# Keys projected by kv head, and the twelve NF4 chunks placed 1-8-3 instead of 2-8-2 around the heads

## The reference

```
q = rope(layernorm(x) @ Wq)      32 query heads of 128
k = rope(ctx @ Wk), v = ctx @ Wv  8 kv heads of 128, 4 query heads share one
w = softmax(where(mask, 30*tanh(q.k*MULT/30), -1e30))
x = x + (w @ v) @ Wo
g = layernorm(x)
x = x + (silu(g @ dq(w1).T) * (g @ dq(w2).T)) @ dq(w3).T      hidden size 1376
```

## Time and profile before

| what | us |
|---|---|
| median of 3 runs (lowest, highest) | 897.48 (897.24, 898.55) |
| the profiled execution, its own time | 897.72 |
| its span, first to last instruction | 895.9 |
| TensorE busy | 814.8 (91%) |
| VectorE busy | 738.5 (82%) |
| ScalarE busy | 436.6 (49%) |
| GpSimd busy | 368.9 (41%) |
| mean granted TensorE clock | 0.975 of full |

### The profile page before, as it was taken

The page is one execution under the profiler, slowest core; times in us unless marked ns, Lnnn a source line. Parts: engine busy times, 40 slices in busy tenths (PEclk is TensorE's granted clock), DMA queues, the critical chain, the costliest instruction groups (busy, mean ns, idle before and its releaser), DMA issues.

```text
span 895.9 us, 10645 instructions
## 1 busy us (share of the span) xinstructions
PE 814.8 (91%) x3806; PEld 645.6 (72%) x3806; DVE 738.5 (82%) x857; ACT 436.6 (49%) x521; POOL 368.9 (41%) x208
## 2 busy tenths in 40 slices
PE   3588798799899999999999999999768999998998
PEld 2466586677677787677777777777546788887886
DVE  8799978599899989999999998898787799895120
ACT  0044466465565565665665566555642365462100
POOL 3445428534634735645536527435001335444000
PEclk9999899899999999999999999999888999999999
DMA  8455564632333432432523433322101311303210
GB/s 323 135 155 145 167 201 106 183 107 80 112 106 83 140 100 72 147 83 71 167 71 87 146 92 97 113 70 80 59 1 33 103 48 54 106 1 104 56 59 36
DMA packets 61940, 91.82 MB, mean 102 GB/s; under 512 B 6720, under 2 KB 28352, under 8 KB 61888
## 3 DMA queue, kind: packets, MB, share of 16 engines
q1 hardware_dynamic: 61888, 91.14, 34.5%
HBM read 51.00 MB, written 19.14 MB: 78 GB/s over the span
## 4 chain that ended last, share of the span: by engine, by line
PE 51%; DVE 25%; issue 9%; DMA 5%; ACT 5%; POOL 3%; SPq 1%; POOLq 0%; DVEq 0%; ACTq 0%
PE bank L454 5%; PE bank L456 5%; PE bank L455 5%; PE bank L545 3%; PE bank L490 3%; PE bank L491 3%; PE bank L474 3%; PE bank L492 3%; PE bank L472 3%; PE bank L473 3%; ACT nfp L690 3%; DVE nfa L856 3%; PE trp L461 3%; PE avp L556 2%; DVE nfx L856 2%
## 5 line engine op out<-in xcount | busy, mean ns | idle before, releaser
L1141 POOL TENSOR_TENSOR qT<-cs_loop,sw 128x512 f32<-128x512 f32 x58 | 82.0, 1414 | 234.2 <-DMA sw<-cs_loop 234.2
L856 DVE SCALAR_TENSOR_TENSOR nfv<-nfp,nfv 128x1408 f32<-128x1408 uint8 x70 | 134.4, 1920 | 18.8 <-ACT nfp L690 16.8
L738 ACT ACTIVATE bank<-bank 128x512 f32<-128x512 f32 x64 | 37.2, 582 | 176.7 <-PE bank L545 176.7
L690 ACT ACTIVATE nfp<-nfv,bnd 128x1408 uint8<-128x1408 f32 x75 | 107.2, 1465 | 23.0 <-POOL nfv L1157 11.4
L856 DVE SCALAR_TENSOR_TENSOR nfa<-nfp,nfa 128x1408 f32<-128x1408 uint8 x56 | 100.3, 1790 | 14.3 <-ACT nfp L690 13.7
L490 PE MATMUL bank<-woh,ath 128*128 128x512 f32 x256 | 109.8, 429 | 0.0
L690 ACT ACTIVATE nfp<-nfa,bnd 128x1408 uint8<-128x1408 f32 x75 | 106.7, 1464 | 5.9 <-POOL nfa L1157 3.6
L472 PE MATMUL bank<-xh,wqh 128*128 128x512 f32 x256 | 106.0, 414 | 0.0
L491 PE MATMUL bank<-wol,ath 128*128 128x512 f32 x256 | 103.6, 405 | 0.0
L492 PE MATMUL bank<-woh,atl 128*128 128x512 f32 x256 | 103.6, 405 | 0.0
L474 PE MATMUL bank<-xh,wql 128*128 128x512 f32 x256 | 101.3, 396 | 0.0
(11 more groups left out here) (130 smaller groups left out, 1775.4 us busy)
## 6 DMA issues: line engine op xcount, KB each, us to landing
sw<-cs_loop SPq DMA_DIRECT2D x116, 128.0 KB, 2.3
stage<-wq_pieces SPq DMA_DIRECT2D x32, 256.0 KB, 2.9
stage<-wo_pieces SPq DMA_DIRECT2D x32, 256.0 KB, 3.0
stage<-dq_scratch SPq DMA_DIRECT2D x32, 256.0 KB, 3.1
sw<-cs_start SPq DMA_DIRECT2D x44, 128.0 KB, 2.3
ks_scratch<-qT SPq DMA_DIRECT2D x16, 256.0 KB, 2.5
vs_scratch<-vst SPq DMA_DIRECT2D x16, 256.0 KB, 4.1
kcur<-ks_scratch SPq DMA_DIRECT2D x16, 256.0 KB, 3.7
```

Source lines behind the costliest of these rows:

```text
L690: nc.scalar.activation(nfp[:, n % 2, :], nf_bufs(c)[0][:, :], ACT.Sign, bias=bnd[:, i:i + 1])\
L856: op = nc.vector.scalar_tensor_tensor(acc[:, :], nfp[:, n % 2, :], STEPS[i], acc[:, :], ALU.mult, ALU.add)
```

## The change

It is one change with these parts:

1. **Keys by kv head.** Wk is laid out by kv head; a piece holds one head. Units run over all eight heads with tokens 0 to 511, then over all eight with tokens 512 to 1023. The first unit needs five pieces and takes them one at a time; unit u < 8 then waits for one more piece each.
2. **Splits of the first 28 pieces.** hi is made by ScalarE (`first_hi`), lo by GpSimd for thirteen pieces (`FIRST_POOL`) and by VectorE for fifteen (`first_low`). Most lo of Wk and ctx's second half stand behind a `rope_parts` or a `rope` in the engines' programs.
3. **Order around the keys.** The eight transposes move to u = 10 to 15 and v = 0, 1; mask tables to u = 8; layer norm to u = 5 to 7.
4. **NF4 placement.** No chunk in the keys. Chunk 0 (now a quarter of w3) at v = 0 to 12; chunks 1 to 8 (w1, w2) in heads 0 to 7; chunks 9, 10, 11 (w3) in the FFN at n = 2 to 22 with one more buffer `nfy`. w3's chunks are cut by blocks of columns (`W3_RUNS`), and stored in two DMAs each. SP stores chunk 0 at v = 14 (ahead of `query_swap(4)`), chunk 9 ahead of `weights_in(15)`.
5. **Hidden's hi on ScalarE**, one unit late (`hidden_hi(n - 1)` behind `silu(n)`), instead of on VectorE.
6. **Down** waits for `h_lo` tile by tile.

```diff
+W3_RUNS = [[(0, 5), (21, 27)], [(5, 11), (27, 32)], [(11, 16), (32, 38)], [(16, 21), (38, 43)]]
...
+            nfy = sb("nfy", [128, CH], f32, ffn)
...
+        FIRST_POOL = (0, 3, 6, 8, 10, 12, 14, 16, 18, 20, 22, 24, 26)
...
         def nf_values(v):
-            if v < 4:
-                return 0, range(9 + 6 * v // 4, 9 + 6 * (v + 1) // 4)
-            return 1, range(15 * (v - 7) // 9, 15 * (v - 6) // 9) if v >= 7 else range(0)
+            return range(15 * v // 13, 15 * (v + 1) // 13) if v < 13 else range(0)
...
         def nf_ffn(n):
-            chunk, m = (10, n - 2) if n < 10 else (11, n - 11)
-            return chunk, range(15 * m // 8, 15 * (m + 1) // 8) if 0 <= m < 8 else []
+            return [divmod(k, 15) for k in range(45 * (n - 2) // 21, 45 * (n - 1) // 21)] if n >= 2 else []
...
(SP)
-            for n in range(12):
+            for n in range(5):
                 first_piece(n)
+            sp.dma_start(tab[:, :, :], table_d).then_inc(tab_in, 16)
             sp.dma_start(mt8[:, :], mask_t).then_inc(mask_in, 16)
-            sp.dma_start(tab[:, :, :], table_d).then_inc(tab_in, 16)
-            for n in range(12, 16):
+            for n in range(5, 16):
                 first_piece(n)
...
             for v in range(16):
-                if v == 4:
-                    nf_load(nf_first[:, CH:2 * CH], 1)
+                if v == 13:
+                    nf_load(1)
+                if v == 14:
+                    nf_store(0)
...
+            sp.wait_ge(nf_out, nf_stored(NKV))
+            nf_load(NKV + 2)
             for n in range(4, 2 * HT):
-                if n == 14:
-                    nf_load(nf_first[:, 4 * CH:5 * CH], 11)
-                if n == 16:
-                    nf_store(dq3[:, 2 * CH:3 * CH], 10)
+                if n == 15:
+                    nf_store(NKV + 1)
+                if n == 17:
+                    nf_load(NKV + 3)
                 weights_in(n)
...
(TensorE)
             for u in range(NK):
-                c, half, kvl = u // 8, u % 8 // 4, u % 4
+                half, kv = u // 8, u % 8
+                if u > 0:
+                    split(pe, 5 + u if half == 0 else 16)
                 wait(pe, cs_done, u - 1)
...
+                for k in range(KT):
+                    if u == 0:
+                        split(pe, k + 2)
...
-                if n == 0:
-                    pe.wait_ge(h_lo, 2 * HT)
+                pe.wait_ge(h_lo, units_of(n))
...
(ScalarE)
+            for n in range(16):
+                first_hi(n)
+            for u in range(10, NK):
+                first_token_hi(u - 10)
+                if u >= 12:
+                    first_hi(u + 4)
...
                 silu(n)
-                chunk, bounds = nf_ffn(n)
-                for i in bounds:
-                    nf_above_bound(chunk, i)
+                if n > 0:
+                    hidden_hi(n - 1)
+                for c, i in nf_ffn(n):
+                    nf_above_bound(NKV + 1 + c, i)
+            hidden_hi(2 * HT - 1)
+            for c, i in nf_ffn(2 * HT):
+                nf_above_bound(NKV + 1 + c, i)
...
(VectorE)
+            for n in (1, 2, 4):
+                first_low(n)
...
             for u in range(NK):
                 rope_parts(u, u % 2, tab[:, 0:2, :])
+                if u < 6:
+                    first_low(5 + 2 * u)
+                if u == 5:
                     dve.wait_ge(x_in, 16)
                     for b in range(4):
                         nc.vector.bn_stats(stat[:, b, :], y[:, b, :])
+                if u == 6:
                     ln_moments(0, range(B), 4)
+                if u == 7:
                     ln_rstd(0, range(B))
                     normalise(0, nrm)
                     normalise(1, nrm)
+                if u == 8:
+                    mask_tables()
+                if u >= 10:
+                    token(u - 10)
+                if u in (13, 14):
+                    first_low(2 * u - 9)
+            nf_prepare(0)
...
             def hidden(n):
...
-                dve.wait_ge(h_done, n + 1)
-                nc.vector.tensor_copy(hh[:, t, half * 512:(half + 1) * 512], hf[:, n % 2, :]).then_inc(h_hi, 1)
...
-                if n in (1, 10):
-                    nf_prepare(10 + n // 10)
+                if n in (1, 7, 14):
+                    nf_prepare(NKV + 1 + n // 7)
...
(GpSimd)
-            for n in range(0, 12, 2):
+            for n in (0, 3, 6):
                 first_low(n)
...
+                for n in {0: (8,), 2: (10,), 3: (12,), 5: (14,), 12: (16,), 13: (18,)}.get(u, ()):
+                    first_low(n)
+                if u == 5:
                     power(0, range(B))
+            first_low(20)
+            nf_normalise(0)
+            for n in (22, 24, 26):
                 first_low(n)
...
             for u in range(AHEAD):
                 query_rope(u)
                 if u in (1, 3):
                     for n in (28 + u - 1, 29 + u - 1):
                         low(n % 4, woh0[:, n % 4, :], wol0[:, n % 4, :], n)
+                if u == 3:
+                    nf_rescale(0)
+            nf_normalise(1)
...
-                if n in (9, 18):
-                    nf_rescale(10 + n // 18)
+                if n in (9, 16):
+                    nf_rescale(NKV + 1 + n // 16)
+            nf_rescale(NKV + 3)
```

More of the change, by code:

```diff
@@ L199, in split @@
         def split(eng, n):
-            if isinstance(n, int) and n <= WO0:
-                wait(eng, piece_lo, (n + 1) // 2)
-                wait(eng, piece_lo_dve, n // 2)
+            if n <= WO0:
+                early_pool = len([m for m in range(n) if m in FIRST_POOL])
+                wait(eng, piece_lo, early_pool)
+                wait(eng, piece_lo_dve, n - early_pool)
             else:
-                eng.wait_ge(piece_lo, n - WO0 // 2)
+                eng.wait_ge(piece_lo, n - WO0 + len(FIRST_POOL))
         def source(n):
@@ L401, in head @@
                 if last:
-                    wait(sp, nf_out, 16 * 9)
+                    sp.wait_ge(nf_out, nf_stored(NKV - 1))
                     for n in range(4):
                         weights_in(n)
-                if last:
-                    nf_load(nf_first[:, 3 * CH:4 * CH], kv + 3)
+                    nf_load(NKV + 1)
             def weights_in(n):
@@ L726, in _ @@
                 nc.scalar.activation(vst[:, v % 4, :], prj2[v % 2][:, :], ACT.Copy).then_inc(v_copied, 1)
-                chunk, bounds = nf_values(v)
-                for i in bounds[0:1]:
-                    nf_above_bound(chunk, i)
-                for i in bounds[1:]:
-                    nf_above_bound(chunk, i)
+                if v < 2:
+                    first_token_hi(6 + v)
+                for n in range(20 + 2 * v, 22 + 2 * v) if v < 4 else ():
+                    first_hi(n)
+                for i in nf_values(v):
+                    nf_above_bound(0, i)
                 if 9 <= v < 13:
@@ L986, in _ @@
                     rope_parts(NK + u, u % 2, csq[:, :, :])
-                for i in bounds[1:]:
-                    nf_add(chunk, i)
+            nf_prepare(1)
             def mask(j):
@@ L1107, in _ @@
                 hidden(n)
-                if n in (1, 10):
-                    nf_prepare(10 + n // 10)
-                chunk, bounds = nf_ffn(n)
-                for i in bounds:
-                    nf_add(chunk, i)
+                if n in (1, 7, 14):
+                    nf_prepare(NKV + 1 + n // 7)
+                for c, i in nf_ffn(n):
+                    nf_add(NKV + 1 + c, i)
+            for c, i in nf_ffn(2 * HT):
+                nf_add(NKV + 1 + c, i)
             for n in range(HT):
@@ L1206, in head @@
                     if b == 7 and not last:
[L1207 to L1211 removed]
+                        nf_normalise(kv + 2)
+                    if b == 0 and kv > 0:
+                        nf_rescale(kv)
                     if not last and b < 4:
@@ L1256 @@
              for w in (w1, w2)]
-    parts.append(np.pad(w3.reshape(2, 128, 2 * HID).transpose(1, 0, 2).reshape(128, 4 * HID),
-                        ((0, 0), (0, NFW - 4 * HID))))
-    nf = np.split(np.concatenate(parts, axis=1), 12, axis=1)
-    nf_first, nf_rest = (np.concatenate([nf[c] for c in cs], axis=1) for cs in ([8, 9, 0, 10, 11], range(1, 8)))
+    by_row = np.pad(w3.reshape(2, 128, 43, BLK).transpose(1, 0, 2, 3), ((0, 0), (0, 0), (0, 1), (0, 0)))
+    cols = [[b for lo, hi in runs for b in range(lo, hi)] for runs in W3_RUNS]
+    third = [by_row[:, :, (c + [43])[:11]].reshape(128, CH) for c in cols]
+    nf = np.concatenate([third[0]] + parts + third[1:], axis=1)
     mask = f(np.asarray(mask_1x1xSxS2_bk0)[0, 0].T)
```

283 lines of the change are left out of this document (128 added, 155 removed).

## The result

The changed kernel takes 909.26 us (median of four runs, 907.06 to 911.54) against 897.36 (897.11 to 898.55) before: a ratio of 1.013, 95% interval 1.0098 to 1.0162. The forecast was 900.2, with a range of 889 to 909. The direction was right, the size was not, and the time lies just outside the range.

What follows compares the result with a forecast made beforehand. TensorE was busy 91% and VectorE 82%, so the question was where TensorE waits; in the FFN, VectorE. A gain of 12.8 by head 0 and a loss of 15.5 in the FFN gave +2.7: 900.2 us, range 889 to 909.

Steps and rivals of the forecast that it cites:

- The start: Keys, values and early queries: first matmul about 7.1, first value 71.1, last query ending 138.9, a gain of 14.6 us.
- The second transpose comes at +19.8: Head 0: that transpose comes 19.8 us after the last early query, before 18.1; 1.8 goes back, 12.8 stays gained.
- Heads: The heads themselves: costed at nothing, since the steps are the same and TensorE sets them.
- VectorE is the matter: FFN: VectorE's work from `hf(2)` sums to 122.8 us and sets the down stage's start, a loss of 15.5.
- upper bound of 22: FFN: the largest loss foreseen, 22 us, with slower additions and the full 6 us wait at chunk 9's store.
- Start-up of the first Signs adds 1.5: FFN's beginning: the first Signs' start-up adds 1.5 us to VectorE's sum of work.
- The store of chunk 9: FFN, SP ahead of `weights_in(15)`: TensorE stands 5 to 6 us, VectorE about 4; cost between 0 and 6.
- The tail: FFN's end: the last three bounds follow unit 21, ahead of w3's split; the down stage starts when VectorE is through, 842.4.
- some 12 us after TensorE's last gate product: Sign of being right: the down stage starts that long after the FFN's last gate product.
- VectorE idle in the FFN by over 10 us: Sign of being wrong: VectorE was forecast without idle from n = 6 on.
- The FFN absorbs the third chunk: Rival, VectorE at n = 2 to 22: FFN loss under 12.8, likely 6, kernel faster at 890.7 us; chance 0.28.
- The start gains little: Rival: lows behind ropes, SP's order and the table load leave a gain of 6, not 12.8: 907 us; chance 0.17.

Runs made afterwards that it cites:

- e7: Changed kernel with the load of x behind the swap of key unit 1 and chunk 0's load behind that of unit 5: 911.23 us.
- e6: Changed kernel with SP's store of chunk 0 behind the whole value loop instead of at v = 14: 904.63 us.
- e1: Changed kernel with GpSimd's normalise of chunk 9 ahead of the `hl` of unit 1 instead of behind it: 903.99 us.
- e5: Changed kernel with the reorderings of e1, e2 and e3 together: 891.41 us, ratio 0.9929 to the kernel before.
- e8: Changed kernel without the fifteen bounds of the last chunk, so a quarter of w3 isn't quantised: 899.78 us.
- e4: Changed kernel with the casts of `hidden` back on VectorE, directly behind `hf` (part 5 undone): 909.91 us.
- e2: Changed kernel with SP's store of chunk 9 behind the load of piece 16 instead of ahead of 15: 905.26 us.
- e3: Changed kernel with w3's first two splits ahead of the last three bounds, on ScalarE and VectorE: 905.67 us.
- e10: Changed kernel with the edits of e5 and e6, and the 45 bounds spread over n = 2 to 21 instead of 22: 889.98 us.

## Why the prediction was wrong, point by point

**The start: right.** First matmul, unit 4, first value and last early query were within 1.1 us of the working. The gain at the last early query was 12.7 and not the 14.6 forecast: 1.0 because it came later than said, the rest by the late reading of the time before. The swap behind `x` landed at 24.35, where 23.3 was said, and e7 shows the queueing.

**Head 0: mis-sized.** The step "The second transpose comes at +19.8" measured 23.5 (139.9 to 163.40). Before, it was 18.9 and not 18.1 (152.6 to 171.53), so 4.6 went back where 1.8 was counted. The chain was named, SP's block at v = 14 and a first Sign 10.7 after the last query. The Sign came 14.8 after it (154.73). What was priced too low is the late `swap(4)`: GpSimd's 5.86 wait stands ahead of the normalise. e6 removes it, and TensorE's wait falls from 9.24 to 1.84. The gain at that transpose was 8.1, not 12.8.

**Heads: costed at nothing, gave 4.2 back.** From that transpose to `hf(2)` it took 541.8 before and 537.6 after. That made the total at `hf(2)` 12.3, near the 12.8 forecast, by two errors that cancel: that agreement is luck. In e1 to e5 and e8, with the same code up to there, it took 536.0 to 538.1, so the 4.2 is more than their spread; of the kernel before there is one trace. That trace places most of it: the lead is 8.3 at the fifth transpose and 11.9 at the ninth (232.37 before, 220.44 after), and in between TensorE waited 1.12 and 2.85 for VectorE's `nrm` before (221.56, 232.37) and not at all for it after. Why VectorE was late there was not tried.

**FFN: the step that failed.** "VectorE is the matter", and the sum of 122.8 for its work with 1.5 for the start-up and 4 for n = 12, gave a loss of 15.5; it was 22.4, just past the upper bound of 22. (That bound was added up wrongly: 15.5, 6.8 for slower additions and 2 for the full 6 make 24.3, and the 22.4 lies inside that.) It was wrong on both sides, too much work and too little waiting:

- *VectorE's work* was 109.4 busy, not 122.8. The 42 additions in the stretch take 79.56, 1.89 each, against 58.34 / 28 = 2.08 before. Alone they would take 42 x 1.67 = 70.1, so contention is 9.4 there, not the 16 and 4 counted. The sum also had 45 at 1.63, but the first of each chunk is another operation, and the three took 3.2 together. The copies on ScalarE move `hl` by a unit, and many then meet no addition: with the copies back on VectorE (e4) the same 42 take 87.9, 2.09 each.
- *"Start-up of the first Signs adds 1.5"* was 4.7 (e1). I did not follow `hidden_hi` to what stands behind `hl(1)` on GpSimd. That was the rule to apply: the change adds a wait to GpSimd, and the normalise is queued behind it.
- *The store of chunk 9* was foreseen as a wait of 5 to 6 (it is 4.96), but counted with VectorE's 4, "If VectorE is behind enough, it costs 0". VectorE was not behind; the whole of it counts, 5.4 (e2).
- *The tail* was left to the sum. At the end VectorE had no backlog (it waited 1.18 for a Sign before the last five). Of the 12.8 us, 9.4 are five additions, the two of unit 21 and the three behind unit 22, all ahead of w3's first split. e3 moves three of them and gets 6.1 back. So the sign "some 12 us after TensorE's last gate product" came true by luck: it was to come from VectorE being late all along, and it came from where five bounds stand. A sign of being wrong came too, VectorE idle in the FFN by over 10 us: it was 25.5.

**The rivals.** "The FFN absorbs the third chunk" had 0.28 and a loss of 6 for the chunk. In the kernel as changed it did not happen. In e5, with the first wait down to 0.8, the second gone and the third down to 5.7, the loss is 4.4, so the stage can do the work that this rival said it could. "The start gains little" priced nearly the right time, 907, for a reason that no milestone shows.

**The rule of the Trainium skill** ("SBUF — State Buffer", section "Who interferes with whom") would have put 1.29 on VectorE for each `hl`. The rows here show less, 0.9 beside a pair and 0.9 beside three additions (e4, 5.98 against 5.08), with `hl` itself 1.3 longer. In sum the measured contention was below what either price gives for each `hl`, since most `hl` met nothing: their mean is 1536 ns against 2037 before, and alone one takes 1.29 us.

## What to carry to other kernels

When a cast or a copy is handed to an idler engine and made one step later, list everything that stands behind its consumer on the third engine: here a free copy on ScalarE moved a normalise on GpSimd and stopped TensorE for 4.9 us. A sum of busy times bounds a stage from below and tells nothing of its waits. Here three moved waits brought 18 us back without removing an instruction. Work that nobody waits for yet (a store, the last bounds) belongs behind the loads and splits that the next matmul needs, until it delays the next ones as much.

## What the runs showed of the hardware

**A pause can cost more than its length, and not the same each time.** The windows of the changed kernel right after its three pauses (the third number from the end is the granted clock), a later one in its down stage, then the kernel before right after its pause of 2.45, and the end of a like pause in the timeline of e8:

```profile
710.60:716.00 5.40, 5.34 (x22) 4.76 (x23) 5.30 (x6) 3.32 (x4) 0.98 (x1) 0.73 0.35 100
...
764.70:770.00 5.30, 5.24 (x18) 4.40 (x19) 4.09 (x4) 1.72 (x3) 0.00 (x0) 0.68 0.80 283
...
836.70:841.00 4.30, 4.25 (x12) 3.37 (x13) 0.59 (x1) 0.00 (x0) 2.02 (x1) 0.64 0.02 4
841.00:850.00 9.00, 9.00 (x47) 7.50 (x46) 2.07 (x3) 1.88 (x3) 0.00 (x0) 1.00 0.52 151
...
826.69:831.00 4.31, 4.31 (x12) 3.33 (x13) 0.00 (x0) 0.00 (x0) 0.00 (x0) 0.62 0.06 17
...
829.63 0.50 PE L680 MATMUL bank<-w3h,hh 128*128 128x512 f32 x1 [2.44 <-DVE w3l L1146]
```

After waits of 4.85, 4.96 and 11.74 us the granted clock averages 0.73, 0.68 and 0.64, a mixture of the levels of 1.2 and 2.4 GHz, where it is 1.00 otherwise. Twelve matmuls took 4.3 us at the down start where they take 2.8 when fed, so that pause cost 1.5 more than it lasted. The kernel before lost as much after 2.45 us. But e8 lost nothing after 2.44: its twelve matmuls took 2.85 us (829.63 to 832.48), all at the higher level, and its down stage is 1.5 shorter than that of the kernel before. And behind the same wait of 4.85, with the same code, the matmuls were back at the higher level 2.9 us after the restart in the changed kernel (713.60) and 5.9 after it in e6 (709.43). So the length of a pause, in these runs, does not tell what comes on top of it: it was 0 to 1.5 us after 2.4, and some 1.5 us or, in e6, up to 3 (an estimate, half of the stretch at the lower level) after 4.85. After e1's wait of 0.83 the transposes take 0.63, where the changed kernel's took 1.09 after 4.85.

**Two engines slow each other by unequal amounts.** In e4 a pair of additions took 5.45 beside a normalise of 3.80, where they take 3.35 and 2.55 alone. Three additions took 5.98 beside an `hl` of 2.61, where they take 5.08 (e10) and 1.29 alone. Both sides of a collision get longer: beside an `hl` by 1.3 on GpSimd's side and by 0.9 on VectorE's, the 0.9 that the forecast took from the earlier trace rows; beside a normalise by 1.25 and 2.1.
